# Turned row maxima written straight into the query operand, and a lead of 21 chunks for 22, in a fused attention and FP4 feed-forward block

## The reference

```python
x = L0_attn_inputs                                   # [4, 1024, 128]
xn = _layernorm(x, axis=-1)
x = x + _L0_attn_ref(xn, ...) + _L0_ffn_ref(xn, ...)

# attention: 16 heads of 8, B = 4, S = 1024
q, k, v = split_heads(xn @ Wq + bq), split_heads(xn @ Wk + bk), split_heads(xn @ Wv + bv)
bias = alibi_slopes(H)[:, None, None] * rel          # rel = pos_k - pos_q
scores = einsum('bhqd,bhkd->bhqk', q, k) / sqrt(8) + bias[None]
attn = softmax(scores, axis=-1)
ctx = einsum('bhqk,bhkd->bhqd', attn, v)
out = ctx @ Wo + bo

# feed-forward, inner width 352: both operands of each product in blocks of 16, FP4 and back
h = silu(fp4_linear(x, w_gate)) * fp4_linear(x, w_up)
out = fp4_linear(h, w_down)
```

## Time and profile before

| | |
|---|---|
| Runs | median 824.98 us (824.71 to 826.1, three runs) |
| The profiled execution's own time | 827.07 us |
| Its span on the chip | 825.2 us |
| Mean granted TensorE clock | 0.967 |
| Transfers, mean over the span | 39 GB/s |

### The profile page before, as it was taken

One profiled execution on the slowest core, in us unless ns is written; L12 is line 12 of the kernel. 1 busy time (PEld: TensorE's weight loads), 2 busy tenths in 40 slices (PEclk: granted clock), 3 DMA queues, 4 the chain that ended last, 5 costly groups with the idle time before them and its releaser, 6 DMA issues.

```text
span 825.2 us, 14500 instructions
## 1 busy us (share of the span) xinstructions
PE 742.4 (90%) x4939; PEld 221.1 (27%) x4939; DVE 733.4 (89%) x1338; ACT 665.6 (81%) x1372; POOL 415.0 (50%) x411
## 2 busy tenths in 40 slices
PE   3198999989899999989899999989899999898987
PEld 2011232222232333223132333222232332222223
DVE  8698999999989989899999999999999899999931
ACT  4203988888788988888898989888888889898996
POOL 6447245473536646483545564671634561362551
PEclk9655999999999999999999999999999999999999
DMA  5730001023102002050100102140100100000000
GB/s 149 230 80 2 2 2 54 26 77 78 40 2 41 15 2 77 14 152 5 40 2 4 38 2 91 53 116 2 40 2 2 40 27 2 2 2 2 2 2 26
DMA packets 32848, 31.87 MB, mean 39 GB/s; under 512 B 4360, under 2 KB 26568, under 8 KB 32776
## 3 DMA queue, kind: packets, MB, share of 16 engines
q1 hardware_dynamic: 32776, 30.96, 13.5%
HBM read 15.91 MB, written 15.04 MB: 38 GB/s over the span
## 4 chain that ended last, share of the span: by engine, by line
PE 60%; DVE 26%; ACT 4%; POOL 3%; issue 3%; DMA 2%; SPq 1%; POOLq 0%; ACTq 0%; DVEq 0%
PE mx L1105 22%; PE pv L1133 22%; DVE neg_half L966 20%; PE low L1171 3%; ACT probs L755 3%; PE low L1156 3%; PE low L1150 2%; PE low L1182 2%; PE low L1163 2%; DVE am L935 1%; PE low L1092 1%; DVE ctx_s L987 1%; DVE mb L955 1%; PE low L1144 1%; PE low L1197 1%
## 5 line engine op out<-in xcount | busy, mean ns | idle before, releaser
L966 DVE TENSOR_REDUCE neg_half<-mx 128x1 f32<-128x512 f32 x1024 | 643.8, 681 | 50.5 <-PE mx L1105 43.9
L755 ACT ACTIVATE probs<-low 128x512 f32<-128x512 f32 x1005 | 551.8, 614 | 78.4 <-PE low L1122 67.1
L1105 PE MATMUL mx<-k_op,q_op 51*128 51x512 bf16 x1024 | 335.9, 395 | 58.3 <-DVE neg_half L966 36.7
L1122 PE MATMUL low<-q_op,k_op 53*128 53x512 bf16 x1005 | 316.2, 385 | 0.8 <-DMA q_op<-m_rows 0.8
L1133 PE MATMUL pv<-probs,v_op 128*32 128x512 f32 x2048 | 273.6, 606 | 3.1 <-ACT pv_s L855 1.4
L1105 PEld LDWEIGHTS mx<-k_op,q_op 51*128 51x128 bf16 x1024 | 71.9, 94 | 365.0 <-DVE neg_half L966 298.6
L657 POOL CAST neg_parts<-neg_max 128x16 bf16<-128x16 f32 x31 | 6.8, 220 | 156.0 <-DVE neg_max L972 66.9
L564 POOL TENSOR_SCALAR mb<-mb 128x960 f32<-128x960 f32 (+2 forms) x17 | 58.7, 3456 | 27.2 <-DVE mb L955 25.8
L1122 PEld LDWEIGHTS low<-q_op,k_op 53*128 53x128 bf16 x1005 | 69.0, 93 | 7.6 <-ACT probs L755 5.3
L1133 PEld LDWEIGHTS pv<-probs,v_op 128*32 128x32 f32 x2048 | 40.3, 108 | 88.8 <-ACT probs L755 37.8
L553 POOL TENSOR_TENSOR zb<-hid,inv 128x704 f32<-128x704 f32 x16 | 22.2, 1386 | 54.5 <-DVE inv L950 53.8
(11 more groups left out here) (143 smaller groups left out, 627.6 us busy)
## 6 DMA issues: line engine op xcount, KB each, us to landing
q_op<-q_rows SPq DMA_DIRECT2D x32, 192.0 KB, 3.7
k_op<-k_rows SPq DMA_DIRECT2D x32, 192.0 KB, 4.7
q_rows<-qp SPq DMA_DIRECT2D x8, 384.0 KB, 2.6
k_rows<-kp SPq DMA_DIRECT2D x8, 384.0 KB, 3.0
x_s<-in_L_attn_inputs_dram SPq DMA_DIRECT2D x8, 256.0 KB, 3.6
q_rows<-qp SPq DMA_DIRECT2D x8, 256.0 KB, 2.9
k_rows<-kp SPq DMA_DIRECT2D x8, 256.0 KB, 3.3
out_dram<-o_s SPq DMA_DIRECT2D x7, 256.0 KB, 3.1
```

The costliest lines, as they stand in the source:

```text
L755: nc.scalar.activation(probs[U % 3][:, 2 * g + x, :], bank("exp", U, j), ACT.Exp).then_inc(st_free, 1)
L966: nc.vector.tensor_reduce(neg_half[m % 2][:, i + kh:i + kh + 1], slot("max", pos, kh), AX.X, ALU.max, negate=True).then_inc(mx_free, 1)
L1105: nc.tensor.matmul(slot("max", pos, kh), q, k, start=True, stop=True).then_inc(mx_full, 1)
L1122: nc.tensor.matmul(bank("exp", U, j), k_op[quad][r, g, kt * P:(kt + 1) * P], q_op[quad][r, g, half * HALF:(half + 1) * HALF], start=True, ...
```

## The change

The buffer `m_rows` in memory, the store into it and the wait for the store are gone. SyncE now issues four transfers for a half, one for each pair n of x and g. Each takes 8 rows of `max_t` (2 parts by 4 query tiles, 128 queries each) and writes 2 rows of 512 in `q_op`. For this the columns of `neg_parts` are grouped by head first and part second, where before the part came first, so the cast and the subtraction now write 4 groups of 4 columns with a gap between them. `keep_turn` waits for the transfers of two halves before instead of the store. `LEAD` goes from 22 to 21, which moves each turn one unit later (to the end of unit 8m-2), makes one chunk less before unit 0, and swaps x in `HEAD`.

```diff
-MAX_IN = 16 * 2
+MAX_IN = 16 * 4
-LEAD = 22
+LEAD = 21
@@
-        m_rows = [nc.dram_tensor(f"m_rows{i}", [2, 2, 2, 4, P], BF16, kind="Internal").ap() for i in range(2)]
-        m_out = [sem(f"m_out{i}") for i in range(2)]
@@
+        def part_of(m, c):
+            return neg_parts[m % 2][:].rearrange("p (n c t) -> p n c t", n=4, c=2)[:, :, c, :]
@@ def max_rows(m)
-                sp.dma_start(m_rows[i].rearrange("c x g t q -> (c x g t) q"), max_t[i][:]).then_inc(m_out[i], 16)
-                sp.wait_ge(m_out[i], (m // 2 + 1) * 16)
-                for part in range(2):
-                    sp.dma_start(q_op[quad][ROW_MAX + part:P:XROWS, :, half * HALF:(half + 1) * HALF],
-                                 m_rows[i][part].rearrange("x g t q -> x g (t q)")).then_inc(m_in[i], 16)
+                for n in range(4):
+                    x, g = divmod(n, 2)
+                    r = XROWS * x + ROW_MAX
+                    sp.dma_start(q_op[quad][r:r + 2, g, half * HALF:(half + 1) * HALF],
+                                 max_t[i][8 * n:8 * n + 8, :]).then_inc(m_in[i], 16)
@@ def max_parts(m), on GpSimd
-                link(nc.gpsimd.tensor_copy(neg_parts[m % 2][:, 0:16], neg_max[m % 2][:]))
-                link(nc.gpsimd.tensor_tensor(neg_parts[m % 2][:, 16:32], neg_max[m % 2][:], neg_parts[m % 2][:, 0:16],
+                link(nc.gpsimd.tensor_copy(part_of(m, 0), neg_max[m % 2][:].rearrange("p (n t) -> p n t", n=4)))
+                link(nc.gpsimd.tensor_tensor(part_of(m, 1), neg_max[m % 2][:].rearrange("p (n t) -> p n t", n=4), part_of(m, 0),
                                              ALU.subtract))
@@ def keep_turn(m)
-                    act.wait_ge(m_out[m % 2], m // 2 * 16)
+                    act.wait_ge(m_in[m % 2], m // 2 * MAX_IN)
```

More of the change, by code:

```diff
@@ L975, in reduce_chunk @@
                     dve.wait_ge(max_ok, 1)
-                    link(nc.vector.tensor_copy(neg_parts[m % 2][:, 0:16], neg_max[m % 2][:]))
-                    nc.vector.tensor_tensor(neg_parts[m % 2][:, 16:32], neg_max[m % 2][:], neg_parts[m % 2][:, 0:16],
+                    link(nc.vector.tensor_copy(part_of(m, 0), neg_max[m % 2][:].rearrange("p (n t) -> p n t", n=4)))
+                    nc.vector.tensor_tensor(part_of(m, 1), neg_max[m % 2][:].rearrange("p (n t) -> p n t", n=4), part_of(m, 0),
                                             ALU.subtract).then_inc(parts_max_ok, 1)
```

## The result

The changed kernel takes 859.71 us (median of 6 runs, 856.14 to 862.39) beside 825.09 us for the kernel before on the same chip: ratio 1.0416, 95% interval 1.0388 to 1.0444. That is 34.6 us slower. I had forecast 834.4 with a range up to 846, so the sign was right and the size far off. The profiled execution took 862.39 us.

What follows compares the result with a forecast made beforehand. TensorE and VectorE, waiting for each other, were taken to share the bound. 9.1 + 0.9 + 0.5 - 1.1 = +9.4 us on the profiled 827.07 gave 836.5, or 834.4 us against the runs' median; range 822.5 to 846.

Steps and rivals of the forecast that it cites:

- The window: Handover of maxima, from the turn to the scores that need them: one unit, 2.96 us on average.
- Landing and copy: In the handover: turn's start to the copy's end 0.54 us; landing 1.03 us after the last issue ends.
- Four issues ... I take 2.02: SyncE's four issues per handover take 2.02 us, making a 3.61 us chain and a 0.65 us wait in twenty-eight halves.
- By the two rows of waits I let half of it through: Of 18.2 us of TensorE waiting for maxima, half reaches the time: +9.1 us.
- The Trainium skill's rule: At the handover's issues: by this rule the handover fits its window and nothing waits; the prediction said the trace disagrees.
- Short issues: Rival at the handover: issues cost what the bias rows' do, the chain fits the mean window; 824.3 us, chance 30%.
- Issues that grow with the pieces: Rival at the handover: 0.68 us per issue, waits about 1.4 us in each of 30 halves; 856 us, chance 12%.
- All made up: Rival in the main stretch: TensorE's idle time, 1.3 us per half, absorbs the whole wait; 825 us, chance 8%.
- The last half, +0.9: At the last half's handover, with shorter units, the scores wait 1.44 us instead of 0.57: +0.9 us.
- The start, -1.1: Before the first scores: 21 chunks instead of 22, maxima landing at about 69.85 instead of scores at 70.92: -1.1 us.
- GpSimd costs nothing: Cast and subtraction on GpSimd, behind one more unit's jobs, finish the parts 0.8 us before half 28's turn: no cost.
- SyncE's queue, +0.5: Parts and gathers go ahead of the maxima of halves 3, 18 and 5: +0.5 us for the three.

Runs made afterwards that it cites:

- three21: perhead21 with the first head's scores waiting for three of the four transfers and the fourth head's for the fourth; 845.25 us, ratio 1.0225 to the kernel before.
- issue_forms: Kernel before with 28 extra small SyncE transfers into rows nothing reads, four of each form in a row; its one execution took 825.42 us.
- lastmid21: Changed kernel with only the last half's turn moved from the end to the middle of its unit; 859.96 us, ratio 1.0416 to the kernel before.
- mid21: Changed kernel with every turn in the middle of its unit instead of at its end; 832.85 us, ratio 1.0076 to the kernel before.
- perhead21: Changed kernel with one semaphore per transfer, each head's scores waiting only for their own; 826.65 us, ratio 1.0016 to the kernel before.

## Why the prediction was wrong

- **The window** was right: 2.96 us predicted, 3.02 at half 28.
- **Landing and copy** were nearly right: 1.03 predicted, 1.07 measured; the copy's end at 0.64 after the turn instead of 0.54.
- **"Four issues ... I take 2.02"** is the first step that failed. They took 2.57, with 0.611 each instead of 0.479. I had weighed the destination rows and the cut and gave the source no weight. I had also misread the cut: the loads from memory are 2 by 2 by 512 on both sides, not 4 pieces into 2. Every SBUF-to-SBUF form measured is at 0.58 or more; why is open. The 0.55 us lie wholly behind the end of the window, and so a wait of 0.65 became 1.2.
- **"By the two rows of waits I let half of it through"** is the second. Counting the waits of two engines for each other (112 and 95) does not say what share of a delay is made up, since both kinds seem to belong to one alternating exchange. At three21's dose, which was the wait I had predicted, everything came through; the changed kernel's 34.6 us against 29.9 more of VectorE's waiting and 4.8 less of TensorE's says the same. With the predicted wait and the right share the sum would have been 843.5, my upper bound; with both right, the 37.8 us of the 31 waits in place of 9.1, it comes to 863, 3 above the measurement. That it comes so near is partly luck. In the traces halves 6 to 28 lose 20.5 us against the kernel before (537.3 for 516.8), and 7.5 us of the whole are lost in half 5 and behind the last half's first scores, where the clock fell; the sum has no term for that.
- **The Trainium skill's rule** ("DMA: Bandwidth & Descriptors", section "Issuing engines are not separate DMA queues"), that initiating a DMA is usually small against the DMA, does not hold for these transfers of 2 KB: one issue takes 0.61 us, and four stand for 2.57 us ahead of a landing of 1.07.
- **The rivals.** Short issues (824.3) are refuted by all 128 issues. Issues that grow with the pieces came nearest in time, 856, and had the right picture of the wait (1.4 in each of 30 halves), but its mechanism is refuted by issue_forms, and that its time came near is partly luck: an issue too dear (0.68) and a share too small (three quarters). All made up is refuted by three21.
- **The last half, +0.9**: the wait there became 2.65 on TensorE instead of 0.57, and the clock fell behind it in the profiled execution. This was undersized, by 1.2 us for the wait and some 4 for the clock where it fell.
- **The start, -1.1**: the first scores start at 68.78 instead of 70.92, 1.1 earlier than said. But lastmid21, with the same instructions up to the last half, has them at 70.35, because its first turn came at 65.95 and the changed kernel's at 64.38. Two executions so give 0.6 and 2.1 for the 1.1.
- **GpSimd costs nothing**: right. In half 24 the parts were ready at 657.85 and the turn began at 658.50. It is true only for the turn at the unit's end: in mid21 the turns of halves 24 and 28 waited 1.3 and 1.5 us.
- **SyncE's queue, +0.5**: right in its place and too small. Half 5's rows came 1.1 us late behind the gathers, and behind them the mean granted clock was 0.52 for 7 us. From half 5's first scores to half 6's are 27.3 us, and 23.6 in the kernel before. The other two halves lost nothing that stands out.

## What to carry to other kernels

A transfer's issue time is a term of its own. Take it from an issue of the very same form, in source, destination and cut (transfers of 4 KB and less had 0.26 to 0.63 us here), and count all issues ahead of the one that is waited for. Where several transfers feed operations that come one after another, let each wait for its own: here that undid 33 of 34.6 us with the same transfers. And where two engines alternate and both are nearly always busy (94% and 93% here), let a wait through whole unless a row shows a reserve, whatever the counts of waits say.

## What was not expected of the hardware

- SBUF-to-SBUF transfers of 2 KB take 0.58 to 0.63 us of SyncE's queue each, whether cut in 2, 4 or 8 rows. To or from memory with equal cuts two small forms take 0.26, but the kernel's own loads from memory, also cut equally, 0.48.
- Small transfers issued right behind 192 KB gathers landed after 2.9 us (perhead21) and 4.0 us (mid21) instead of 1.07.
- TensorE's granted clock fell to 0.50 to 0.55 behind the last half's start in some executions of a kernel and not in others of the same one; a value product of 8 matmuls took 1.93 us then instead of 1.06.
